# The second attention of a two-layer kernel as a pipeline over all heads, with three more products a head on TensorE

## The reference

```python
y = layernorm(x) * gamma + beta                 # over the 256 features
q, k = y @ Wq + bq, y @ Wk + bk                 # 8 heads of 32 columns
v = (y @ Wv + bv), summed over its 8 parts      # 256 columns
a = softmax(q_h @ k_h.T / sqrt(32))             # for each sequence and head, 256 x 256
out = a @ v_h                                   # 32 columns a head
```

## Time and profile before

| | us |
|---|---|
| three runs: lowest, median, highest | 2944.11, 2952.01, 2957.39 |
| the profiled execution | 2941.34 |
| its span | 2939.5 |
| `pipeline_one` up to the first line of the layer norm | 0 to 1417 |
| layer norm and weights of the second attention | 1417 to 1471.4 |
| its main block | 1471.4 to 1761.2 |
| `pipeline_two` | 1761.2 to 2939.5 |

### The profile page before, as it was taken

How to read it: one execution, slowest core, us unless ns; L and a number is a source line. 1 busy time by engine, 2 the same in 40 slices (tenths; PEclk the granted TensorE clock), 3 DMA queues, 4 the chain that set the end, 5 groups by cost and what they waited for, 6 DMA issues and landing times. The chain is left out here.

```text
span 2939.5 us, 119767 instructions
## 1 busy us (share of the span) xinstructions
PE 2524.8 (86%) x50858; PEld 2074.4 (71%) x50858; DVE 1973.6 (67%) x7388; ACT 1149.9 (39%) x3661; POOL 430.8 (15%) x404
## 2 busy tenths in 40 slices
PE   1678999999999999885377874899999999999999
PEld 0455677777777777643144543899999999999998
DVE  4557777777777777875745443667677666776665
ACT  3125555555555555562233432233333333333333
POOL 0000000000000000000189100122222222222222
PEclk9678999999999999997656565899999999999999
DMA  5000000000000000000122003000000000000000
GB/s 159 1 2 2 5 5 5 5 5 5 5 5 5 5 5 5 6 4 3 37 97 86 7 16 112 20 8 8 8 9 8 8 10 8 9 11 8 5 5 6
DMA packets 52730, 53.55 MB, mean 18 GB/s; under 512 B 24679, under 2 KB 46840, under 8 KB 50042
## 3 DMA queue, kind: packets, MB, share of 16 engines
q1 hardware_dynamic: 47284, 27.79, 3.5%
q0 software_dynamic: 2000, 14.68, 1.4%
q10 hardware_dynamic: 2934, 3.69, 0.4%
HBM read 39.59 MB, written 6.55 MB: 16 GB/s over the span
## 5 line engine op out<-in xcount | busy, mean ns | idle before, releaser
L103 PE MATMUL p<-g_hl,m_h 128*128 128x128 f16 x3072 | 529.2, 219 | 0.0
L103 PE MATMUL p<-g_hh,m_l 128*128 128x128 f16 x3072 | 529.1, 219 | 0.0
L103 PE MATMUL p<-g_hh,m_h 128*128 128x128 f16 x3072 | 529.1, 219 | 0.0
L765 DVE STREAM_TRANSPOSE gt<-lg_b 128x512 f32<-128x512 f32 x324 | 230.4, 711 | 217.0 <-PE lg_b L448 203.7
L1910 POOL TENSOR_TENSOR a_l<-a,a_h 128x384 f16<-128x384 f32 x256 | 234.1, 914 | 918.2 <-ACT a_h L1868 918.2
L657 ACT ACTIVATE hm<-xy,b 128x512 f32<-128x512 f32 x512 | 348.0, 680 | 0.1
L642 ACT ACTIVATE gl<-gt 128x128 f32<-128x128 f32 x324 | 100.2, 309 | 629.0 <-DVE gt L765 628.9
L103 PEld LDWEIGHTS p<-g_hh,m_h 128*128 128x128 f16 x3072 | 300.5, 98 | 1.8
L103 PEld LDWEIGHTS p<-g_hh,m_l 128*128 128x128 f16 x3072 | 300.7, 98 | 0.7
L103 PEld LDWEIGHTS p<-g_hl,m_h 128*128 128x128 f16 x3072 | 300.9, 98 | 0.0
L448 PE MATMUL lg_b<-a_wh_hi,lh 128*32 128x256 f16 x4096 | 217.7, 291 | 78.8 <-DVE lh L789 76.7
(11 more groups left out here) (421 smaller groups left out, 7105.5 us busy)
## 6 DMA issues: line engine op xcount, KB each, us to landing
m_stage<-in_m_w POOLq DMA_DIRECT2D x12, 1024.0 KB, 5.3
hs<-in_m_w SPq DMA_DIRECT2D x16, 384.0 KB, 3.2
xs<-in_x POOLq DMA_DIRECT2D x1, 2048.0 KB, 8.5
x_dram<-x SPq DMA_DIRECT2D x16, 128.0 KB, 2.2
s_v<-in_l_wv SPq DMA_DIRECT2D x1, 2048.0 KB
attention_dram<-att SPq DMA_DIRECT2D x16, 128.0 KB, 2.8
attr<-attention_dram SPq DMA_DIRECT2D x128, 16.0 KB, 1.8
x2r<-x_dram SPq DMA_DIRECT2D x16, 128.0 KB, 2.5
```

Of the source, the lines that this page charges most:

```text
L103: ins = pe.matmul(out, w[wp](k), x[xp](k), start=start, stop=last and k == KT - 1 and xp == 1, skip_group_check=True)
L765: dve.transpose(gt[:, :], lg_b[slot // QS % 2][:, :, :, :].rearrange("p g a x -> p (g a x)"))\
```

## The change

The main block of `attention_two` is written anew, and its results stay the same:

- No loop: the 64 heads run through as one list, g = 0 to 63, with `b` and `h` worked out when the program is built. The block that set the semaphores and wrote the banks is gone, and so are the writes of zeros ahead of the layer norm.
- There are four score banks in place of two. `scores(p)` makes a pair of heads: the products of the two heads alternate, one on rows r to r+31 of the array and one on the next 32. PE runs the pair for heads g+2 and g+3 in step g, ahead of `values(g-2)`.
- The projections share one bank (`pj`), except for batch 0. Their six halves are spread over steps 0, 1, 3, 5 and 6 of a batch (`PROJECT_AT`), two halves in step 3; the high parts follow on ACT (`HIGH_AT`) and the low parts on DVE. `xn`, q, k, v and `sums` are there twice. The last batch projects nothing.
- The bias row and the ones are a tile of 128 rows, all but two of them zero in the bias.
- DVE makes the row maxima two heads ahead and splits the input for batch b+2 in steps 4 (high) and 6 (low).
- `turn` first makes three products of the constant weights `w_hi["q"]`, 256 columns each, into the bank that the transposes overwrite. They stand ahead of the wait for the exponentials and behind the wait for `pt_lo`; nobody reads them.
- In the layer norm `sq`, `yy` and `y` use memory of `prob`, `att` and `root`, and its banks are the score banks.

```diff
+GH = B * NH
+PROJECT_AT = {0: ((0, 0),), 1: ((0, 1),), 3: ((1, 0), (1, 1)), 5: ((2, 0),), 6: ((2, 1),)}
+HIGH_AT = {2: 0, 4: 1, 7: 2}
...
-        brow = sb("brow2", [2, 3 * D], F16)
+        brow = sb("brow2", [P, 3 * D], F16)
...
-        sc = [ctx.enter_context(nc.psum_tensor(f"sc{j}", [P, TT, BT], F32)) for j in range(2)]
+        sc = [ctx.enter_context(nc.psum_tensor(f"sc{j}", [P, TT, BT], F32)) for j in range(4)]
...
-        pq, pk, pv = (ctx.enter_context(nc.psum_tensor(n, [P, TT, BT], F32)) for n in ("pq", "pk", "pv"))
+        pj = ctx.enter_context(nc.psum_tensor("pj", [P, TT, BT], F32))
+
+        def pj_bank(b, j):
+
+            return (sc[2], sc[3], pj)[j] if b == 0 else pj
...
-        with nc.Block() as block:
-            @block.sync
-            def _(sp):
-                for s, n in per:
-                    sp.sem_inc(s, n)
...
+            def project(b, j, half):
+
+                bank = pj_bank(b, j)
+                if half == 0:
+                    pe.wait_ge(xn_split, 2 * (b + 1))
+                    if b > 0:
+                        pe.wait_ge(pj_lo, 3 * b + j)
...
+            def scores(p):
+
+                b, m, r = p // 4, p % 4 // 2, 2 * DK * (p % 2)
+                if p % 4 == 0:
+                    pe.wait_ge(pj_lo, 3 * b + 2)
+                if p >= 2:
+                    pe.wait_ge(exp_done, 2 * (2 * p - 2))
...
                 for s_ in range(TT):
+                    for q, k in ((qh, kh), (ql, kh), (qh, kl)):
+                        for e in range(2):
+                            r0 = r + e * DK
+                            last = pe.matmul(sc[2 * (p % 2) + e][:, s_, :], q[r0:r0 + DK, m, s_ * P:(s_ + 1) * P],
+                                             k[r0:r0 + DK, m, :], start=(s_ == 0 and k is kh and q is qh),
+                                             stop=(k is kl), skip_group_check=True, tile_position=(r0, 0))
                 last.then_inc(sc_pe, 1)
...
+            def turn(g):
+                if g >= 2:
+                    pe.wait_ge(pt_lo, g - 1)
+                for _ in range(3):
+                    pe.matmul(pt[g % 2][:, 0, :], w_hi["q"][:, 0, 0:P], w_hi["q"][:, 0, :], start=True, stop=True,
+                              skip_group_check=True)
+                pe.wait_ge(exp_done, 2 * (g + 1))
                 first = True
...
+            for j in range(3):
+                for half in range(2):
+                    project(0, j, half)
+            scores(0)
+            for g in range(GH + 2):
+                b, h = g // NH, g % NH
+                if 1 <= g <= GH:
+                    turn(g - 1)
+                if g % 2 == 0 and g // 2 + 1 < GH // 2:
+                    scores(g // 2 + 1)
+                if g >= 2:
+                    values(g - 2)
+                for j, half in PROJECT_AT.get(h, ()):
+                    if b + 1 < B:
+                        project(b + 1, j, half)
...
+            for g in range(GH + 1):
+                b, h = g // NH, g % NH
+                if g < GH:
+                    exps(g)
+                if g >= 1:
+                    high(g - 1)
+                if h in HIGH_AT and b + 1 < B:
+                    projected(b + 1, HIGH_AT[h])
...
+            for g in range(GH + 2):
+                b, h = g // NH, g % NH
+                if 2 <= g:
+                    low(g - 2)
+                if g % 2 == 1 and g + 2 < GH:
+                    row_max(g + 2)
+                if h == 0 and b > 0:
+                    inverse(b - 1)
+                    if b < B:
+                        projected(b, 2)
+                elif h == 1 and b > 0:
+                    finish(b - 1)
+                elif h in (3, 5) and b + 1 < B:
+                    projected(b + 1, h // 2 - 1)
+                elif h in (4, 6) and b + 2 < B:
+                    split_x(b + 2, h // 2 - 2)
+                if g % 2 == 0 and g + 2 < GH:
+                    row_max(g + 2)
```

More of the change, by code:

```diff
@@ L1239, in _ @@
             rows = attd[0:B * T * D].rearrange("(b h s p j) -> b p h s j", h=NH, s=TT, p=P, j=HV)
-            with sp.Fori(0, B) as b:
-                sp.wait_ge(att_done, at(b, 1, 2))
+            for b in range(B):
+                sp.wait_ge(att_done, b + 1)
                 for s_ in range(TT):
-                    sp.dma_start(rows[bass.ds(b, 1), :, :, s_, :].rearrange("o p h j -> (o p) h j"),
-                                 att[:, :, s_, :]).then_inc(att_sent, 16)
-            sp.wait_ge(att_sent, 16 * TT * (B + 2))
+                    sp.dma_start(rows[b, :, :, s_, :], att[:, :, s_, :]).then_inc(att_sent, 16)
@@ L1273, in scores @@
-            def scores(b, h):
-                r0, m = DK * (h % 4), h // 4
-                if h == 0:
-                    pe.wait_ge(qk_split, at(b, 2, 2))
-                pe.wait_ge(exp_done, at(b, 2 * NH, 2 * (h - 1)))
-                for s_ in range(TT):
-                    for q, k in ((q_h, k_h), (q_l, k_h), (q_h, k_l)):
-                        last = pe.matmul(sc[h % 2][:, s_, :], q[r0:r0 + DK, m, s_ * P:(s_ + 1) * P],
-                                         k[r0:r0 + DK, m, :], start=(s_ == 0 and k is k_h and q is q_h),
-                                         stop=(k is k_l), skip_group_check=True, tile_position=(r0, 0))
-                last.then_inc(sc_pe, 1)
@@ L1309, in values @@
                                              stop=(u == TT - 1 and pp is pt_l), skip_group_check=True)
                 last.then_inc(pv_pe, 1)
-            project(0)
-            with pe.Fori(0, B) as b:
-                for h in range(NH):
-                    if h > 0:
-                        scores(b, h)
-                    turn(b, h - 1)
-                    values(b, h - 3)
-                    if h == 0:
-                        scores(b, h)
-                    if h == 4:
-                        project(b + 1)
@@ L1323, in _ @@
-            turn(B, -1)
-            for h in (-3, -2, -1):
-                values(B, h)
+            for j in range(3):
[13 more added lines that the diff above has]
+                        project(b + 1, j, half)
@@ L1364, in _, with exps @@
-            high(B, -2)
-            high(B, -1)
+            def exps(g):
+                b, h = g // NH, g % NH
+                act.wait_ge(neg_max, g + 1)
+                if g >= 2:
+                    act.wait_ge(t_pe, g - 1)
+                if h == 0 and b >= 2:
+                    act.wait_ge(r_done, b - 1)
+                for s_ in range(TT):
+                    act.activation(prob[:, g % 2, s_, :], sc[g % 4][:, s_, :], ACT.Exp, bias=nmax[:, g % 4, s_:s_ + 1],
+                                   accum_out=sums[:, b % 2, h, s_:s_ + 1]).then_inc(exp_done, 1)
@@ new lines, in high, with projected @@
+            def high(g):
+                act.wait_ge(t_pe, g + 1)
+                if g >= 2:
+                    act.wait_ge(pv_pe, g - 1)
+                act.activation(flat(pt_h[:, g % 2]), flat(pt[g % 2][:, :, :]), ACT.Copy).then_inc(pt_hi, 1)
+            def projected(b, j):
+                act.wait_ge(pj_full, 3 * b + j + 1)
+                if b >= 2 and j < 2:
+                    act.wait_ge(sc_pe, 4 * (b - 1))
+                elif b >= 2:
+                    act.wait_ge(pv_pe, NH * (b - 1))
+                act.activation(flat((q_h, k_h, v_h)[j][b % 2][:, :, :]), flat(pj_bank(b, j)[:, :, :]), ACT.Copy,
+                               scale=PJ_SCALE[j]).then_inc(pj_hi, 1)
@@ L1422, in _ @@
-            inverse(B)
-            low(B, -2)
-            low(B, -1)
-            finish(B)
+            split_x(0, 0)
+            split_x(0, 1)
+            for j in range(2):
+                projected(0, j)
+            row_max(0)
+            row_max(1)
+            projected(0, 2)
+            split_x(1, 0)
+            split_x(1, 1)
+            for g in range(GH + 2):
+                b, h = g // NH, g % NH
+                if 2 <= g:
[14 more added lines that the diff above has]
+                    row_max(g + 2)
```

221 lines of the change are left out of this document (86 added, 135 removed).

## The result

| | before | changed |
|---|---|---|
| median (lowest to highest), us | 2952.91 (2944.11 to 2957.39), 4 runs | 2822.68 (2816.53 to 2835.60), 4 runs |
| profiled execution, its span | 2941.34, 2939.5 | 2822.39, 2820.3 |
| main block (first split to the end of the last finish) | 285.46 | 170.67 |

The ratio is 0.9568 (95% interval 0.9528 to 0.9608): 130 us less between the medians, 119 between the two profiled executions. I had forecast 2868, with a range down to 2842, so the gain is 45 us larger than forecast and lies outside the range.

A forecast was written before the change was run, and what follows sets the result against it. PE was taken to bound the stage, idling 62 us and mostly at 1.2 GHz. List 166.5, stalls 19.5 and ends 22 make 208 us, 84 less: 2857, with 10.7 for the median 2868 us; range 2842 to 2915.

The forecast's parts named there:

- The clock: TensorE in the stage: full clock for three quarters of the work, falls behind long splits; list 166.5 us.
- Full clock throughout: Rival for the whole stage: 187.4 us, 104 us less, 2848; no chance of its own stated.
- the class of 0.55: Outcome for the whole kernel: full clock for most of the list, 2840 to 2880 us, chance 0.55.
- Stalls: PE behind DVE's splits, 21 us, and waiting for bank pj, 5 us: 26 us at full clock, 19.5 used.
- The pair: PE's work for two heads with its projection share: 4.50 us at full clock, 8.02 at half.
- The ring: Scores, row maximum, exponentials, transposes: with row maxima two heads ahead, exponentials are ready when PE comes to them.
- Ends: Before the first transpose 14 us, after the last step 8 us, 22 us together.
- Fillers charged in full: Constant products ahead of the wait for exponentials: 0.66 us a pair at full clock, 1.28 at half, none counted free.
- The rule on transposes: TensorE clock: full clock doesn't engage for transpose-mode, so transposes are dead time and the outcome leans to the half-clock sum.
- half clock throughout, 2930: Rival for the stage: fillers don't lift the clock, PE bounds all the time; 22 us less, chance 0.08.
- Slower, 2982: Rival in every even step: a pair's scores don't run beside each other at half clock; 30 us more, chance 0.05.
- The median: Whole kernel: median of the three runs shown lies 10.7 us above the profiled execution, making 2857 into 2868.

The follow-up runs named there:

- the rewrite: Changed kernel with the bias on two rows and without the three constant products a head, the list written anew alone: 2848.52 us, ratio 0.9658.
- the run with GpSimd away: Changed kernel with GpSimd's splits of the expert weights held until the last batch of attention is finished: 2964.22 us, block 5.3 us shorter.
- the run with later scores: Changed kernel with a pair's scores (heads g+1, g+2) in odd step g: 2882.96 us, ratio 0.9797; also without constant products: 2893.16 us, ratio 0.9795.
- the kernel with the earlier reading: Changed kernel with ACT and DVE reading bank pj one step earlier for q and k: 2810.02 us, ratio 0.9532.

## Why the prediction was wrong, point by point

- **The clock: the step that failed.** I had "full clock for three quarters of the work, with falls behind the long splits": 166.5 us for the list. From the trace after: 7 x 17.79 us (19.43 less two waits of 0.82) and 12.73, together 137.3. That is within 2 us of the full-clock sum of 139.4, and it is 29 us of the miss. The quarter at half clock would have been 62 us; some 14 us of the block were. Two things were wrong in it. First, I expected falls behind every long split; one pair of splits made a stretch like this, and the clock fell at its end:

```profile
1552.00:1557.00 5.00, 1.14 (x19) 0.74 (x17) 5.00 (x7) 1.90 (x7) 4.85 (x3) 0.98 0.02 7
```

  Second, I saw the clock stay at 0.50 for 20 us with PE busy 19.81 and asked for no cause; in that window stood 2-row bias products with a gap of 0.2 us at each half. I took the tile "at nothing beyond this run of seven"; alone it gives 29 us in the kernel before, and of the rewrite's 0.73 it makes 0.90. It isn't the whole answer: the three products make 0.92 of the same 0.73, and waits put back into PE's list bring the clock down again, to 0.87 with the products and 0.70 without. So the clock hung on three things together, the list without waits, the bias tile and the products, and the quarter was a guess with no row behind it.
- **Full clock throughout.** This rival came nearest. I had given it no chance of its own: its 2848 lay in the class of 0.55, and what came had 0.03 as "faster than 2840". Its sum of 187.4 us was still 13 too long, 10 of them stalls.
- **Stalls: mis-sized.** 26 us at full clock, 19.5 as used. Measured 16: 4.4 for the one long batch (the fall of the clock behind the split is in it), 11.4 for the bank (I had 5: 0.6 a batch; it was 0.82 twice a batch, since q and k both wait; without it the kernel is 11.3 us faster). My own sign of being wrong, that PE waits elsewhere than behind the split, came true here. The split stalls, put at 3.5 us in each of six batches, came to 5.3 us in all by the run with GpSimd away. Halves of 2.17 us (twice) fit into PE's slack of a step: those batches took 19.43 like the others. I had charged each.
- **The pair: right, in part by luck.** 4.50 us forecast at full clock, 17.79 / 4 = 4.45 measured. Scores 0.76 (0.90 taken, 0.75 the lower bound), fillers 0.64 (0.66), transposes 0.97 (1.00), values 0.73 over a batch (0.78), projections 1.16 (1.16). These add up to 4.26; the other 0.19 is PE standing ahead of `values` for `pt_l`, which twice a batch makes 0.82 of the 0.44 us from the transposes on. I had no such term, and scores taken 0.14 too long made up for most of it. A slip in the half-clock sum, 0.35 added for the 0.32 just worked out, is worth 1 us in 32 pairs.
- **The ring: right in its result, its way only half seen.** Scores to exponentials to transposes was named; the run with later scores shows that the arm that bites in the new list is the row maximum on DVE with `low` behind it.
- **Ends: right as a remainder.** 22 forecast; 174.0 - 137.3 - 16 = 20.7.
- **Fillers charged in full: right as a length, too much as a price.** 192 x 0.11 = 21 us as I charged them; without them the kernel is only 7 us faster: two batches at full clock gain 1.66 us each, two with a fall lose 1.6, and the long one is gone (19.39 for 23.87). The rival in which they "don't lift it" was half true: they lift nothing in the kernel before, and in the new list they hold it.
- **The rule on transposes.** By the Trainium skill (TensorE: Matmul & The Clock Gate, part 4), as I cited it, the outcome leaned towards half clock throughout, 2930. Here the list with 32 transposes a batch (4 x 0.97 = 3.9 of its 19.43 us) stood at 1.00 for batch after batch. No run here takes the transposes apart from the rest, so the rule itself is neither shown nor refuted; as a guide to the outcome it misled.
- **Slower, 2982.** It needed scores that don't run beside each other. They do, even when they aren't alternated.
- **The median, by luck of one run.** I carried over that the profiled run of before lay 10.7 us below its median. The changed kernel's lies 0.3 below. The miss of 45 us is 35 us between profiles (34 of them the stage, 208 against 174) and 10 of this.

Of what should show it: stage 210 and clock 0.85 came out at 174 and 0.95 (by my own sum, 62 of 166.5 us at half clock, the list's clock would have been 0.81); the pair, the wait for exponentials, the 12 scores (the last starts 0.56 us after the first) and `pipeline_two` (1178.3 us before, 1179.5 after) as written; idle time behind every split did not show.

## What to carry to other kernels

Ask of a list at half clock not only how busy PE is but what stands between its products: with 2-row products and the gaps around them 42 products in a row stayed at half clock in four profiles of five, and with 128 rows the clock rose after some 3 to 6 us in all 13. Products that fill waits gave nothing in the kernel before, with a clock of 0.62, held the clock in the new list where waits were left (0.87 against 0.70), and cost 7 us once the waits were few. So put them in and take them out again after each rewrite, and measure both. Once PE sets the pace, every wait left on it (here 0.82 us, 14 times) comes off one for one, until the next engine is full.

## What the hardware showed that I had not expected

- A half projection with a 2-row bias product took 1.72 us at half clock and 0.97 at full, with a 128-row one 1.49 and 0.77. More rows of zeros are cheaper.
- PE busy 0.87 of the block at a clock of 0.63 (kernel before with constant products), and 0.70 of it at 0.87 (scores later): busy share alone doesn't tell the clock.
- Products on two groups of 32 rows overlap even when six of one stand ahead of six of the other: the second group's started 0.24 us after the first's first product.
- The same copy of the input took 0.62 us with GpSimd idle and up to 5.80 beside it in the changed kernel, and in the kernel with the earlier reading it alternated between 2.45 and 3.15 from batch to batch. DVE's instructions that read PSUM kept their length beside GpSimd: `pt_l` took 682 ns on average with it and 683 without, the row maximum 684 and 685.
